# A running maximum that begins with two chunks at once, in a graph network on one core

## The reference

```
scores = einsum('hbnd,hbdm->hbnm', f_self, f_other)
masked = a_h * scores
masked = where(masked >= 0, masked, 0.2 * masked) / sqrt(16)
masked = masked + where(a_h == 0, -1e9, 0.0)
attn   = softmax(masked, axis=-1) * (a_h != 0)
x      = layernorm(x + relu(attn @ feats + bias))
x      = layernorm(x + ((adj + I) @ x) / rowsum(adj + I))
x      = layernorm(x + adj @ (x @ weight) + bias2)
x      = layernorm(x + where(adj @ x > 0.5, 1, 0))
```

## Time and profile before

| what | value |
|---|---|
| median of three runs | 1534.63 us |
| the profiled execution | 1531.98 us, span 1529.9 us |
| TensorE matmul busy | 1343.7 us, 88% |
| VectorE busy | 1266.8 us, 83% |
| ScalarE busy | 1223.3 us, 80% |
| GpSimd busy | 1035.5 us, 68% |
| mean granted TensorE clock | 0.946 of full speed |

### The profile page before, as it was taken

The page is one execution under the profiler, slowest core; times in us unless marked ns, Lnnn a source line. Parts: engine busy times, 40 slices in busy tenths (PEclk is TensorE's granted clock), DMA queues, the critical chain, the costliest instruction groups (busy, mean ns, idle before and its releaser), DMA issues. The chain is left out here.

```text
span 1529.9 us, 21041 instructions
## 1 busy us (share of the span) xinstructions
PE 1343.7 (88%) x7296; PEld 675.7 (44%) x7296; DVE 1266.8 (83%) x1490; ACT 1223.3 (80%) x1404; POOL 1035.5 (68%) x562
## 2 busy tenths in 40 slices
PE   2788889998989988999989989999889999899856
PEld 1443334544445544444545544454445444355323
DVE  2677998897888889898888889988898988988864
ACT  1587888887988878898888878988788888888731
POOL 3067777787677776778677776778767776867412
PEclk7898999999999999999999999999999999999978
DMA  6624552434424442425325344245424343200000
GB/s 94 111 34 63 61 79 52 68 41 48 90 43 63 57 65 56 54 61 52 72 62 75 34 49 89 45 60 59 66 62 58 53 47 69 54 15 16 26 10 11
DMA packets 140879, 84.95 MB, mean 56 GB/s; under 512 B 100372, under 2 KB 130522, under 8 KB 140762
## 3 DMA queue, kind: packets, MB, share of 16 engines
q1 hardware_dynamic: 125542, 64.67, 20.1%
q0 software_dynamic: 14160, 18.51, 15.6%
q10 hardware_dynamic: 1072, 0.43, 0.1%
HBM read 103.33 MB, written 21.38 MB: 82 GB/s over the span
## 5 line engine op out<-in xcount | busy, mean ns | idle before, releaser
L533 POOL TENSOR_TENSOR LS<-LS,MB 125x1000 f32<-125x1000 f32 x372 | 860.7, 2332 | 368.2 <-DVE LS L934 272.2
L774 ACT ACTIVATE LS<-Z 126x1000 f32<-126x1000 f32 x576 | 575.1, 1000 | 150.6 <-PE Z L601 149.9
L782 ACT ACTIVATE LS<-LS 125x1000 f32<-125x1000 f32 x576 | 595.8, 1035 | 47.3 <-POOL LS L533 22.5
L920 DVE TENSOR_TENSOR RP<-LS,RP 125x1000 f32<-125x1000 f32 x480 | 575.6, 1199 | 45.0 <-ACT LS L774 19.4
L599 PE MATMUL Z<-AT,BI 126*126 126x500 fp8e4 x1152 | 367.2, 401 | 77.8 <-ACT LS L774 44.2
L601 PE MATMUL Z<-FS,FO 128*125 128x500 f16 x1152 | 348.8, 384 | 0.0
L628 PE MATMUL M<-LS,V 126*18 126x500 f32 x2304 | 315.9, 622 | 8.8 <-ACT LS L782 8.7
L934 DVE TENSOR_TENSOR LS<-LS,MB 125x1000 f32<-125x1000 f32 x204 | 319.9, 1573 | 0.1
L599 PEld LDWEIGHTS Z<-AT,BI 126*126 126x126 bf16 x1152 | 126.8, 138 | 376.6 <-issue 158.2
L683 PE MATMUL M<-AT,XP 125*128 125x500 fp8e4 x756 | 203.4, 378 | 3.6 <-ACTq L821 3.1
L601 PEld LDWEIGHTS Z<-FS,FO 128*125 128x125 f16 x1152 | 162.0, 141 | 92.4 <-issue 9.2
(11 more groups left out here) (133 smaller groups left out, 798.7 us busy)
## 6 DMA issues: line engine op xcount, KB each, us to landing
MB<-row_maxima SPq DMA_DIRECT2D x48, 500.0 KB, 4.1
adj_cast<-in_adj_dram POOLq DMA_DIRECT2D x96, 183.1 KB, 4.5
FO<-PARTS SPq DMA_DIRECT2D x120, 46.9 KB, 2.1
FS<-PARTS SPq DMA_DIRECT2D x120, 46.9 KB, 2.1
XF<-in_x_dram SPq DMA_DIRECT2D x8, 336.0 KB
XA<-in_x_dram SPq DMA_DIRECT2D x8, 336.0 KB
out_dram<-X SPq DMA_DIRECT2D x7, 375.0 KB
AT<-adj_cast SPq DMA_TRANSPOSE x144, 2.8
```

What stands on the lines that cost most here:

```text
L533: nc.gpsimd.tensor_tensor(rows, rows, MB[:P, u % 2, :, :], ALU.subtract).then_inc(sub_pool, 1)
L774: nc.scalar.activation(LS[:PD, q % RL, :, :], banks("Z", q)[:PD], ACT.Prelu, alpha=SLOPE).then_inc(bent, 1)
L782: nc.scalar.activation(rows, rows, ACT.Exp, scale=0.25).then_inc(exps, 1)
L920: nc.vector.tensor_tensor(run, rows, run, ALU.max).then_inc(maxed, 1)
```

## The change

The first two chunks of a unit are taken together: at m = 0 nothing is done, and at m = 1 one `scalar_tensor_tensor` takes the maximum of chunk 0, the floor and chunk 1, reads both chunks from `LS` and writes `RP`. The semaphore `maxed` is raised by two there, so all later counts stay as they were. The other edits let `power`, `low` and the waits on them be cut into `HALVES` parts; `HALVES` is 1, and the steps at which they run are unchanged. The diff, cut to its core:

```diff
+HALVES = 1
+POWERS = ((28, 49, 66, 89),)
+LOWS = ((30, 50, 70),)
...
-            def power(b, l):
+            def power(b, l, k):
+                part = RSTD[:, NT // HALVES * k:NT // HALVES * (k + 1)]
                 pool.wait_ge(var_ok, 4 * b + l + 1)
-                nc.gpsimd.tensor_tensor(RSTD[:, :], RSTD[:, :], NHALF[:, :], ALU.pow).then_inc(rstd_ok, 1)
+                nc.gpsimd.tensor_tensor(part, part, NHALF[:, 0:NT // HALVES], ALU.pow).then_inc(rstd_ok, 1)
...
             for q in range(END):
-                if layer_at(q, LOW):
-                    low(*layer_at(q, LOW))
-                if layer_at(q, POWER):
-                    power(*layer_at(q, POWER))
+                for k in range(HALVES):
+                    if layer_at(q, LOWS[k]):
+                        low(*layer_at(q, LOWS[k]), k)
+                for k in range(HALVES):
+                    if layer_at(q, POWERS[k]):
+                        power(*layer_at(q, POWERS[k]), k)
...
-                    pe.wait_ge(xp_ready, 3 * b + l + 1)
+                if part * HALVES % CUTS == 0:
+                    pe.wait_ge(xp_ready, HALVES * (3 * b + l) + part * HALVES // CUTS + 1)
...
             def maximum(q):
                 u, m = divmod(q, STEPS)
+                if m == 0:
+                    return
                 dve.wait_ge(bent, q + 1)
                 rows, run = LS[:P, q % RL, :, :], RP[:P, :, 0:C]
-                if q:
-                    dve.wait_ge(maxed, q)
-                if m == 0:
-                    nc.vector.tensor_scalar(run, rows, FLOOR, None, ALU.max).then_inc(maxed, 1)
+                if q > 1:
+                    dve.wait_ge(maxed, q - (m == 1))
+                if m == 1:
+                    nc.vector.scalar_tensor_tensor(out=run, in0=LS[:P, (q - 1) % RL, :, :], scalar=FLOOR, in1=rows,
+                                                   op0=ALU.max, op1=ALU.max).then_inc(maxed, 2)
                 elif m == STEPS - 1:
...
-                dve.wait_ge(rstd_ok, 4 * b + l + 1)
+                dve.wait_ge(rstd_ok, HALVES * (4 * b + l + 1))
```

More of the change, by code:

```diff
@@ L55 @@
 SUM = (26, 46, 66, 88)
-POWER = (28, 49, 66, 89)
 SCALE = (28, 49, 67, 90)
 HIGH = (29, 51, 69)
-LOW = (30, 50, 70)
 COLLECT = ((33, 34, 35, 36, 37, 38, 39, 40, 41, 42, 43, 44),
@@ L533, in subtract, with low @@
                 nc.gpsimd.tensor_tensor(rows, rows, MB[:P, u % 2, :, :], ALU.subtract).then_inc(sub_pool, 1)
-            def power(b, l):
+            def power(b, l, k):
+                part = RSTD[:, NT // HALVES * k:NT // HALVES * (k + 1)]
                 pool.wait_ge(var_ok, 4 * b + l + 1)
-                nc.gpsimd.tensor_tensor(RSTD[:, :], RSTD[:, :], NHALF[:, :], ALU.pow).then_inc(rstd_ok, 1)
-            def low(b, l):
+                nc.gpsimd.tensor_tensor(part, part, NHALF[:, 0:NT // HALVES], ALU.pow).then_inc(rstd_ok, 1)
+            def low(b, l, k):
+                tiles = slice(NT // HALVES * k, NT // HALVES * (k + 1))
                 pool.wait_ge(xh_ready, 3 * b + l + 1)
-                nc.gpsimd.tensor_tensor(XP[:, :, F:2 * F], X[:, :, :], XP[:, :, 0:F], ALU.subtract).then_inc(xp_ready, 1)
+                nc.gpsimd.tensor_tensor(XP[:, tiles, F:2 * F], X[:, tiles, :], XP[:, tiles, 0:F], ALU.subtract).then_inc(xp_ready, 1)
             for q in range(END):
-                if layer_at(q, LOW):
-                    low(*layer_at(q, LOW))
-                if layer_at(q, POWER):
-                    power(*layer_at(q, POWER))
+                for k in range(HALVES):
[4 more added lines that the diff above has]
+                        power(*layer_at(q, POWERS[k]), k)
                 e = q - POOL_AT
```

## The result

The changed kernel takes 1555.65 us (median of three runs, 1552.19 to 1555.9) against 1534.63 before: a ratio of 1.0135, 95% interval 1.0116 to 1.0153, 21.0 us more where 19.4 were forecast.

What follows compares the result with a forecast made beforehand. No engine is full; a loop of waits through TensorE, ScalarE, GpSimd and VectorE sets the pace. Profiled 1531.98 + 19.7 (6.7 + 5.6 + 7.4) + 2.65 to the median gives 1554 us, range 1538 to 1566.

Steps and rivals of the forecast that it cites:

- The split does nothing: Whole kernel: with `HALVES` 1 each loop runs once over the whole tile, same waits and counts; no effect.
- Two SBUF inputs exclude GpSimd, a PSUM destination changes nothing: New maximum in every unit: waits out GpSimd's operation, ends 1.06 us after it, takes 1.20 to 3.34 us.
- Rivals 1 and 2: New operation never waits for GpSimd: nothing gained, 1534 to 1535 us (0.10); or 16 us gained, 1518 us (0.08).
- B, 6 x 1.1 = 6.7 us: Second unit of each graph: new operation waits for GpSimd, ScalarE's square comes 1.1 us later, six times: 6.7 us.
- C, 7 x 0.8 = 5.6 us: Third unit of each graph: GpSimd's second subtraction goes first, `row_maxima` is 0.8 us late, seven times: 5.6 us.
- rival 3: Third unit of each graph: new operation gets in ahead of GpSimd and costs nothing there; 1549 us, chance 0.17.
- E, 7 x 1.06 = 7.4 us: Fifth unit of each graph: GpSimd's subtraction, awaited by ScalarE's exponential, moves by 1.06 us, seven times: 7.4 us.
- The sign that I had named: Fifth unit of each graph: ScalarE's exponential would wait about 1.1 us longer.
- A, D, F at nothing: First, fourth and sixth units: changes fall into VectorE's wait for TensorE and GpSimd's idle time; no cost.
- No gain from 57 us less of VectorE work: All units: VectorE loses 48 x 1.20 = 57 us of work, but other waits take it up; nothing gained.
- rival 4: Whole kernel: TensorE regains half of the 19.7 us; 1544 us, chance 0.13.

Runs made afterwards that it cites:

- e1: Changed kernel with the first chunk left out, the operation reading the second chunk from SBUF and RP's old content from PSUM: 1531.57 us, ratio 0.9985.
- e2: New operation in the first, fourth and sixth units of each graph alone, the old pair in the others: 1535.83 us, ratio 1.0016.
- e5: New operation in the second unit of each graph alone, the old pair in the others: 1545.26 us, ratio 1.0084.
- e6: New operation in the third unit of each graph alone, the old pair in the others: 1539.78 us, ratio 1.0038.
- e4: Changed kernel with the floor copy of the first chunk put back, its result overwritten by the new operation: 1563.45 us, ratio 1.0209.
- e8: Changed kernel measured once more, unchanged, beside the kernels with the operation in single units: 1557.70 us, ratio 1.0151 to the kernel before.

## Why the prediction was right, and where its terms were off

- *The split does nothing*: instruction counts agree but for VectorE's 48 fewer (1490 to 1442). Not tested by itself.
- *Two SBUF inputs exclude GpSimd, a PSUM destination changes nothing*: right. The new operations took 1.20 to 3.32 us, the upper bound having been 3.34, and e1, which has one SBUF input and the same destination, shows that the inputs decide. Rivals 1 and 2, which start from an operation that never waits, fall with it. The rule of the Trainium skill ("SBUF — State Buffer", "Who interferes with whom") that a VectorE instruction with two SBUF inputs and a GpSimd one reading SBUF block each other held for this form too, in both directions: 3.30 us in C, where GpSimd was first, and 5.58 us for GpSimd's pair in F, where VectorE was.
- *B, 6 x 1.1 = 6.7 us* (the product is 6.6): the mechanism right link by link, the size too small. The wait alone is 1.03 us a unit, but alone in the kernel the six operations cost 12.9 us (interval 9.5 to 16.1), since in its trace four units in which the clock halves grow by 2.6 to 3.9 us. In the two traces of the changed kernel the six units come to 10.4 and 10.0 us. The term left the clock out.
- *C, 7 x 0.8 = 5.6 us*: right; 5.8 us (3.1 to 8.7), 0.8 to 1.1 us a unit in the changed kernel. GpSimd did go first, so rival 3 falls.
- *E, 7 x 1.06 = 7.4 us*: too large; 4.9 us (2.8 to 7.2), in most graphs 0.47 us a unit. I took the row from unit 22, the one graph in which GpSimd's low part began without a wait for ScalarE; unit 40 has 0.26 us of wait there, and part of the delay goes into it. Unit 22 was an exception altogether: the low part began 7.9 us after the unit's first bend, in the other six E units 6.9, and the unit was 1.06 us longer than in e2, e5 and e6, which leave E as it was. The sign that I had named, an exponential that waits 1.1 us longer, came out as 0.48 us in unit 40.
- *A, D, F at nothing*: nearly; 0.16% (0.02 to 0.29). The median units keep their length; where the 0.16% lie is not shown.
- *No gain from 57 us less of VectorE work*: nearly right; e1 finds 2.5 us. But e4 shows that this holds beside the old order alone: with the exclusion there, an L914 more costs 9 to 11 us by the ratios, more than E did.
- *TensorE regains part* (rival 4): no; the delays in B, C and E stand in the lengths of the units and in the total.

So the mechanism was right, but that the forecast came within 2 us was in part luck. Measured alone the terms are 12.9 + 5.8 + 4.9 against 6.7 + 5.6 + 7.4: B's was 6.2 us too small and E's 2.5 us too large, which offset each other in part, and e8, the same kernel again, came out 23.1 us slower by the ratio and not 21.0.

## What to carry to other kernels

Before joining two operations, look at where their inputs lie: an accumulator in PSUM kept VectorE's maximum out of GpSimd's way, and one operation fewer with both inputs in SBUF cost more than two with one each. When two engines exclude each other, judge the place by what waits behind either of them, its next excluded operation included, not by the first consumer alone. Take a row for a repeated pattern from more than one of its repeats.

## What the runs showed of the hardware that was not expected

Of TensorE's clock: in the kernels with the operation in B an extra wait of 1.1 us for ScalarE was followed by half the clock in 15 of 30 units, in those without it at the same place in none. In units 13 to 37 a B unit grew by 2.3 to 3.9 us where that happened, and by 0.7 to 1.1 us, with one exception, where it did not.

The exclusion adds little of its own: a VectorE operation that had to wait was done 1.06 to 1.07 us after GpSimd's end, against 1.20 us unhindered, and GpSimd's low part in E 1.50 us after VectorE's end, against 1.65.
